# Attention phase of an AdaLN block: k projected from plain codes and scaled in place, softmax and v in fp16 halves, q's sine products swapped by transfers, instructions in a new order

## The reference

```python
def _dequant(codes, scales):                       # GS = 128: one scale per 128 input rows and output column
    w = codes.astype(jnp.float32) - 8.0
    return w * jnp.repeat(scales, GS, axis=0)

def _rope(x):
    ...
    re = xe * cos - xo * sin
    ro = xo * cos + xe * sin
q = hidden_states @ _dequant(q_codes, q_scales)
...
```

## Time and profile before

| | |
|---|---|
| time, median of 3 runs (lowest, highest) | 1821.96 us (1821.85, 1822.86) |
| the profiled execution's own time | 1821.32 us |
| its span | 1819.5 us, 34099 instructions |
| PE busy | 1767.9 us (97%) |
| PEld busy | 1019.7 us (56%) |
| DVE busy | 1378.0 us (76%) |
| ACT busy | 1223.1 us (67%) |
| POOL busy | 692.2 us (38%) |
| mean granted PE clock | 0.987 |

### The profile page before, as it was taken

How to read it: one execution, slowest core, us unless ns; L and a number is a source line. 1 busy time by engine, 2 the same in 40 slices (tenths; PEclk the granted TensorE clock), 3 DMA queues, 4 the chain that set the end, 5 groups by cost and what they waited for, 6 DMA issues and landing times. The chain is left out here.

```text
span 1819.5 us, 34099 instructions
## 1 busy us (share of the span) xinstructions
PE 1767.9 (97%) x14143; PEld 1019.7 (56%) x14143; DVE 1378.0 (76%) x2104; ACT 1223.1 (67%) x2090; POOL 692.2 (38%) x501
## 2 busy tenths in 40 slices
PE   8889999999999999999999999999999999689998
PEld 7845555555555555555555555555555555256665
DVE  4657777777777777777777777777777777389997
ACT  2257777777777777777777777777777777522222
POOL 1144334433443344334433443344333333133332
PEclk9999999999999999999999999999999999789999
DMA  6100010001000100010001000100000000412221
GB/s 252 38 33 24 12 36 1 24 13 36 1 24 13 36 1 24 13 36 1 24 13 36 1 24 13 36 1 24 13 1 2 1 1 1 151 47 74 79 82 47
DMA packets 24039, 58.70 MB, mean 32 GB/s; under 512 B 7256, under 2 KB 7768, under 8 KB 22608
## 3 DMA queue, kind: packets, MB, share of 16 engines
q1 hardware_dynamic: 23888, 56.55, 9.4%
HBM read 47.61 MB, written 8.93 MB: 31 GB/s over the span
## 5 line engine op out<-in xcount | busy, mean ns | idle before, releaser
L840 ACT ACTIVATE banks<-banks,ratios 128x512 f32<-128x512 f32 x768 | 476.1, 658 | 137.8 <-PE banks L612 137.4
L612 PE MATMUL banks<-o_hl,w_o 128*128 128x512 f16 x2048 | 532.2, 382 | 6.4 <-DVE o_hl L731 4.5
L536 PE MATMUL banks<-hT,w_q 128*128 128x512 f16 x2048 | 527.6, 380 | 7.3 <-DVE q_sin L688 4.0
L835 ACT ACTIVATE banks<-banks,ratios 128x512 f32<-128x512 f32 x768 | 492.8, 665 | 26.1 <-PE banks L536 15.4
L789 POOL TENSOR_TENSOR q_f<-q_f,q_sin 128x1024 f32<-128x1024 f32 x128 | 301.1, 2352 | 294.5 <-DVE q_sin L688 294.5
L612 PEld LDWEIGHTS banks<-o_hl,w_o 128*128 128x128 f16 x2048 | 187.4, 98 | 243.7 <-DVE accT L741 17.1
L688 DVE TENSOR_TENSOR q_sin<-banks,rope_q 64x1024 f32<-64x1024 f32 x256 | 312.8, 1222 | 13.3 <-POOL q_f L789 8.0
L536 PEld LDWEIGHTS banks<-hT,w_q 128*128 128x128 f16 x2048 | 191.6, 98 | 229.6 <-ACT banks L835 6.0
L845 ACT ACTIVATE o_hl<-banks 128x512 f16<-128x512 f32 x256 | 138.9, 595 | 144.8 <-PE banks L596 144.8
L741 DVE SCALAR_TENSOR_TENSOR accT<-banks,scales,accT 128x512 f32<-128x512 f32 x224 | 158.0, 746 | 60.8 <-PE banks L612 55.0
L563 PEld LDWEIGHTS banks<-w_kv,hT 128*128 128x128 f16 x3072 | 182.2, 98 | 30.1
(11 more groups left out here) (117 smaller groups left out, 1639.3 us busy)
## 6 DMA issues: line engine op xcount, KB each, us to landing
codes<-in_codes SPq DMA_DIRECT2D x40, 512.0 KB, 3.7
accT<-in_xT SPq DMA_DIRECT2D x8, 1024.0 KB, 12.3
x_f<-in_x SPq DMA_DIRECT2D x32, 256.0 KB, 3.0
out<-res SPq DMA_DIRECT2D x32, 256.0 KB, 2.1
kv_s<-in_kv_scales SPq DMA_DIRECT2D x8, 512.0 KB, 4.8
hT<-aggb_rows SPq DMA_DIRECT2D x1, 2048.0 KB, 12.8
hT<-in_base_T SPq DMA_DIRECT2D x1, 1024.0 KB, 5.9
aggw_rows<-agg_sb SPq DMA_DIRECT2D x1, 512.0 KB, 2.7
```

Of the source, the lines that this page charges most:

```text
L536: mm = pe.matmul(banks[:, tile], w_q[:, n[2], kt * RF * HD + tile * HD:kt * RF * HD + (tile + 1) * HD], hT[:, kt, hp, t0:t0 + CHUNK], star ...
L612: mm = pe.matmul(o_bank(t), w_o[:, p[2], h * D + tile * P:h * D + (tile + 1) * P], o_hl[:, op, h], start=h == 0 and op == 0, stop=op == 1, ...
L835: act.activation(banks[:, tile], banks[:, tile], ACT.Copy, scale=ratio(0, n, tile, kt)).then_inc(q_scaled[tile], 1)
L840: act.activation(o_bank(t), o_bank(t), ACT.Copy, scale=ratio(1, p, 2 * pair + t, h)).then_inc(o_scaled, 1)
```

## The change

- k's weights become plain codes minus 8 in fp16 (`make_k`: one POOL instruction where four were). `project_k` does 2 matmuls for a kt, 8 in all, and DVE multiplies `kv_bank` by the ratio in place between them (`scale_k`, 3 a step); the last scale is in the tables `rope_k`.
- `move_v` writes only the high fp16 half of v, and DVE writes the low one (`v_low`). The softmax is split as well: ACT writes the high half (`p_high`), POOL the low one (`p_low`), DVE transposes both in one instruction of 1024 fp16 elements. `values` does 3 fp16 matmuls where one f32 matmul was.
- `turn_sin` is one instruction of 128 partitions that leaves the products where they are. SP moves each half of the partitions to the other with two DMAs (`swap_q`) into a new tile `q_swap`, and `add_q` waits for them. `q_sin` and `q_swap` are single buffers, so the swap of one pair waits for the addition of the other.
- Every engine's order in `body` is rewritten; semaphores are split by tile or bank. SP issues one code piece a step (`load`) between the swaps.

The diff, cut to its core:

```diff
-    def make_kv(self, pool, g, which):
...
+    def make_k(self, pool, g):
+        self.wait_piece(pool, g, 0)
+        pool.tensor_scalar(self.k[:, g % 2], self.codes[:, 0, 0:KT * HD], -8.0, 1.0, ALU.add, ALU.mult)
...
+        def swap_q(n, pair):
+
+            sp.wait_ge(q_sin_done[pair], at(n) + 1)
+            if pair or at(n):
+
+                sp.wait_ge(q_ready[1 - pair], at(n) + pair)
+            for h in range(2):
+                sp.dma_start(q_swap[64 * h:64 * (h + 1)], q_sin[64 * (1 - h):64 * (2 - h)]).then_inc(q_swapped[pair], 16)
...
+        def body(n, i, p):
+            if n:
+                load(n)
+            if i:
+                swap_q(i, 1)
+            if n:
+                swap_q(n, 0)
...
+        def project_k(n, kt):
+            t0 = n[1] * CHUNK
+            if kt:
+                pe.wait_ge(k_scaled, 3 * at(n) + kt)
...
+            for hp in range(2):
+                mm = pe.matmul(kv_bank, w.k[:, n[2], kt * HD:(kt + 1) * HD], hT[:, kt, hp, t0:t0 + CHUNK],
+                               start=kt == 0 and hp == 0, stop=hp == 1, skip_group_check=True)
             mm.then_inc(k_psum, 1)
...
             for j in range(CT):
                 for b in (2 * half, 2 * half + 1):
-                    if half and j == 0:
-                        pe.wait_ge(out_ready, TB * at(i) + b - 1)
-                    mm = pe.matmul(o_bank(b)[:, j * P:(j + 1) * P], v_f[b * S:(b + 1) * S, i[1] % 2, j],
-                                   pT[b * S:(b + 1) * S, j * P:(j + 1) * P], start=True, stop=True, skip_group_check=True)
+                    rows = slice(b * S, (b + 1) * S)
+                    for m, (vp, pp) in enumerate(PASSES):
+                        mm = pe.matmul(o_bank(b)[:, j * P:(j + 1) * P], v_hl[rows, p[1] % 2, vp, j],
+                                       pT_hl[rows, pp, j * P:(j + 1) * P], start=m == 0, stop=m == 2, skip_group_check=True)
...
+        def scale_k(n, kt):
+            dve.wait_ge(k_psum, KT * at(n) + kt + 1)
+            dve.tensor_scalar(kv_bank, kv_bank, w.ratios[:, n[0], K_ROW, kt:kt + 1], None, ALU.mult).then_inc(k_scaled, 1)
...
         def turn_sin(n, pair):
+            if n[1] == 0 and n[0]:
+                dve.wait_ge(w_ready, n[0])
 
             if pair or at(n):
-                dve.wait_ge(q_ready[1 - pair], at(n) + pair)
-            for h in range(2):
-                ins = turn(n, pair, 1, slice(64 * (1 - h), 64 * (2 - h)), q_sin[64 * h:64 * (h + 1)])
-            ins.then_inc(q_products[pair], 1)
...
+                dve.wait_ge(q_swapped[1 - pair], 32 * (at(n) + pair))
+            turn(n, pair, 1, slice(0, P), q_sin[:]).then_inc(q_sin_done[pair], 1)
...
+            dve.transpose(pT_hl[:].rearrange("p a t -> p (a t)"), p_hl[:].rearrange("p a t -> p (a t)")).then_inc(probs_T, 1)
...
+        def v_low(n):
+            dve.wait_ge(v_hi, at(n) + 1)
+            hi, lo = (v_hl[:, n[1] % 2, part].rearrange("p j d -> p (j d)") for part in range(2))
+            dve.scalar_tensor_tensor(out=lo, in0=kv_bank, scalar=1 / WSCALE, in1=hi, op0=ALU.mult, op1=ALU.subtract).then_inc(v_ready, 1)
...
         def add_q(n, pair):
-            pool.wait_ge(q_products[pair], at(n) + 1)
+            pool.wait_ge(q_cos_done[pair], at(n) + 1)
+            pool.wait_ge(q_swapped[pair], 32 * at(n) + 32)
             q = q_f[:, 2 * pair:2 * pair + 2]
-            pool.tensor_tensor(q, q, q_sin[:], ALU.add).then_inc(q_ready[pair], 1)
+            pool.tensor_tensor(q, q, q_swap[:], ALU.add).then_inc(q_ready[pair], 1)
...
+        def p_low(i):
+            pool.wait_ge(p_hi, at(i) + 1)
+            pool.tensor_tensor(p_hl[:, 1], sc[:], p_hl[:, 0], ALU.subtract).then_inc(p_ready, 1)
...
+        def p_high(i):
+            act.wait_ge(probs, at(i) + 1)
+            act.activation(p_hl[:, 0], sc[:], ACT.Copy).then_inc(p_hi, 1)
```

More of the change, by code:

```diff
@@ L258, in _ @@
         sp.dma_start(aggb_rows, agg_sb[:, S * S:]).then_inc(agg_stored, 16)
-        w.load(sp, a, 0)
+        for j in range(PIECES):
+            w.load_piece(sp, a, 0, j)
         sp.wait_ge(agg_stored, 32)
@@ L583, in scores, with values @@
             mm.then_inc(scores_psum, 1)
-        def values(i, half):
+        def values(p, half):
             if half == 0:
-                pe.wait_ge(probs_T, at(i) + 1)
-                pe.wait_ge(v_ready, at(i) + 1)
-                if at(i):
-                    pe.wait_ge(acc_added, NT * at(i))
+                pe.wait_ge(probs_T, at(p) + 1)
+                pe.wait_ge(v_ready, at(p) + 1)
+                if at(p):
+                    for tile in (2, 3):
+                        pe.wait_ge(acc_added[tile], at(p))
+            else:
+                for b in range(2):
+                    pe.wait_ge(out_ready[b], at(p) + 1)
@@ L598, in values @@
                     if j == CT - 1:
-                        mm.then_inc(pv_psum, 1)
-        def output(p, pair, h):
-            if h == 0 and pair == 0:
-                pe.wait_ge(out_ready, TB * at(p) + TB)
-            for t in range(2):
-                tile = 2 * pair + t
-                if h:
-                    pe.wait_ge(o_scaled, 12 * at(p) + 6 * pair + 2 * (h - 1) + t + 1)
-                elif pair:
-                    pe.wait_ge(acc_added, NT * at(p) + t + 1)
-                for op in range(2):
-                    mm = pe.matmul(o_bank(t), w_o[:, p[2], h * D + tile * P:h * D + (tile + 1) * P], o_hl[:, op, h],
-                                   start=h == 0 and op == 0, stop=op == 1, skip_group_check=True)
-                mm.then_inc(o_psum, 1)
+                        mm.then_inc(pv_psum[half], 1)
@@ new lines, in output @@
+        def output(p, tile, h):
+            if h:
+                pe.wait_ge(o_scaled[tile], 3 * at(p) + h)
+            else:
+                for b in range(TB):
+                    pe.wait_ge(out_ready[b], at(p) + 1)
+                if tile >= 2:
+                    pe.wait_ge(acc_added[tile - 2], at(p) + 1)
+            for op in range(2):
+                mm = pe.matmul(o_bank(tile), w.o[:, p[2], h * D + tile * P:h * D + (tile + 1) * P], o_hl[:, op, h],
+                               start=h == 0 and op == 0, stop=op == 1, skip_group_check=True)
+            mm.then_inc(o_psum[tile], 1)
@@ L750, in body @@
             if i:
-                turn_sin(i, 1)
+                turn_cos(i, 1)
+                v_low(i)
             if p:
+                out_low(p, 3)
                 out_low(p, 2)
-                out_low(p, 3)
             if n:
-                rotate_k_sin(n)
+                scale_k(n, 0)
+            if i:
+                scores_T(i)
+            if n:
+                scale_k(n, 1)
             if i:
                 softmax_max(i)
+            if n:
+                scale_k(n, 2)
             if p:
+                add_out(p, 1)
                 add_out(p, 0)
-                add_out(p, 1)
+            if i:
+                softmax_sum(i)
             if n:
@@ L774, in body @@
             if p:
+                add_out(p, 3)
                 add_out(p, 2)
-                add_out(p, 3)
         program(body)
@@ L822, in body @@
                 normalize(i)
-                if i[0] < NKV - 1:
-                    dequantize(i)
+                p_low(i)
         program(body)
         pool.wait_ge(v_psum, STEPS)
+        for tile in range(RF):
+            pool.wait_ge(q_psum[tile], KT * STEPS)
         pool.memset(mixw_f, 0.0).then_inc(mixw_zeroed, 1)
```

390 lines of the change are left out of this document (218 added, 172 removed).

## The result

The changed kernel takes 1976.93 us (median of 4 runs, 1974.96 to 1979.53), the kernel before 1822.19 us (4 runs, 1821.85 to 1822.86). The ratio is 1.0853, with a 95% interval from 1.0839 to 1.0867. Predicted were 1787 us, with a range from 1762 to 1828.

The account below looks back on a forecast made before the run. The prediction took PE to be the bound, without holes. A step would go from 22.81 to 22.24 us; 63 steps give -36 us, the ends +2, so 1787 us, range 1762 to 1828.

Parts of the forecast that it names:

- Nearest: 2.7 ... so I take 2.7: loop 20.8, cover 1.4: Swap time taken from a 512 KB store out of SBUF, 2.7 us, giving a loop of 20.8 us with 1.4 cover.
- D: Time of one swap of q's sine products between partition halves, by two DMAs; taken as 2.7 us, bounds 2.1 to 3.7.
- 15.4 + 2D, hidden for D up to 3.4: Loop from one step's scores to the next's, through both swaps: 15.4 us plus 2D, hidden under the 22.24 us step.
- Rival 4: The swap loop is the bound, from D = 3.4; 1822 us at 3.7, 1860 at 4.0; chance 0.10.
- two slots for three matmuls: Values blocks on PE: fp16 matmuls of two sequences partly overlap, 1.10 us a block against the old 1.09, change 0.
- always two side by side: Lower bound for a values block on PE, row groups fully overlapping: 0.87 us, or -0.44 us a step.
- Rival 2: Values blocks on PE run fully side by side, -0.44 us a step: 1759 us; chance 0.08.
- Rival 3: Values on PE: fp16 blocks of 32 rows do not overlap, +0.90 us a step: 1845 us; chance 0.12.
- 4 x 0.2165 = 0.87: k on PE: 12 matmuls become 8, saving 0.87 us a step.
- Holes 0.3: Waits on PE in the new order, at output heads, scale_k, add_out and unseen places: 0.3 us a step.
- Rival 5: The new order opens more holes on PE, 0.7 instead of 0.3 us a step: 1813 us; chance 0.13.
- Ends +2: First step and end of the kernel, outside the steady steps: +2 us in all.

Follow-up runs that it names:

- e2_half_columns: The changed kernel with each swap DMA moving one of the pair's two tiles, half of the bytes: 1785.54 us.
- e4_filled_wait: The changed kernel with nine more mask matmuls on PE ahead of its wait in front of the scores: 1930.15 us.
- e10_no_transfer: The changed kernel without the swap transfers, the rotation add taking the sine product as it lies, other work the same: 1761.57 us.
- e7_values_f32: The kernel of e6_scores_later with the values part undone, one f32 matmul again and no v_low, p_high, p_low: 1818.40 us.
- the third pass: The kernel of e6_scores_later with a third matmul, with weights of zero, in each of a step's four k passes: 1811.10 us.
- e6_scores_later: The changed kernel reordered: last passes of q tiles 1 and 0, an output and a k pass ahead of the scores, turn_sin and scale_k ahead of scores_T: 1780.87 us.
- e9_two_queues: The changed kernel with the second DMA of each swap issued by ScalarE's queue, in time with the first: 2014.74 us.

## Why the prediction was wrong, step by step

**The step that failed: "Nearest: 2.7 ... so I take 2.7: loop 20.8, cover 1.4".** D was 4.35 us and 4.32 (medians; means 4.41 and 4.52). The bounds, 2.1 to 3.7, did not hold it either, so the range could not. The rows behind them were of one DMA each, with one end outside SBUF; the swap is two DMAs one behind the other, the second 0.50 later, and both move out of and into SBUF. Each row was a time to landing, and none of a pair. What the Trainium skill gives ("DMA: Bandwidth & Descriptors", Anatomy of one DMA), 2.0 us plus bytes / 436e3, is a fit for transfers that GpSimd issues, while SyncE issues these. As an estimate it agrees with the halved transfers (128 KB: 2.3 by both) and not with the full ones: 2.6 for the first 256 KB against 3.1, 3.2 for the pair against 4.2. The measurement decides.

**The loop, "15.4 + 2D, hidden for D up to 3.4".** The mechanism was right, and its size nearly so. Between 400 and 1400 us 22 steps of the changed kernel have the full clock. In each of them the step less its two D is 15.62 to 15.72 us, mean 15.64, though D goes from 4.2 to 5.5: the step follows both D one for one. With D = 3.2 (e2_half_columns) the step is 22.17, just above PE's 21.88. By the measured sizes the loop is hidden up to (21.88 - 15.64) / 2 = 3.1. Rival 4 had the right place and price (13 us for 0.1) and nearly the threshold, and a chance of 0.10 because its D ended at 4.0. By its own formula D = 4.35 gives 15.4 + 8.7 = 24.1 and 1821 + 63 x 1.29 + 2 = 1904 us. To the measured 1977 some 73 are missing. 0.24 us a step that the loop is longer are 15 of them, 0.23 that the mean D is above 4.35 are another 15, and the clock is some 41.

**Not in the prediction at all: the clock.** It took the full clock of the earlier trace rows for granted. It falls in some of the steps whose waits in front of the scores are 2.4 to 4.1 us long, and that costs some 41 us (0.64 us a step; e4_filled_wait, without it, is 47 us faster). Neither did the prediction have the swaps of 4.95 to 5.55 us, ten of 79. Only two of them have a code load beside them, and their cause stays open.

**PE's sum.** For each part, in us a step from start to start, what the prediction had, and what e10_no_transfer has over before (mask and scores, 1.32 in both, are left out of the rows but not of the step):

| part | before | predicted | measured | after |
|---|---|---|---|---|
| k | 2.60 | -0.87 | -0.54 | 2.06 |
| values | 2.18 | 0 | -0.62 | 1.56 |
| output | 6.92 | | +0.21 | 7.13 |
| v | 2.68 | | +0.10 | 2.78 |
| q | 7.10 | | -0.08 | 7.02 |
| holes, all parts | | +0.3 | in the rows above | |
| step | 22.81 | 22.24 | | 21.88 |

- **Values, "two slots for three matmuls".** Wrong, and on the safe side. 24 fp16 matmuls on 32 rows take 0.78 us, less than the 0.87 for "always two side by side", though the order is three and three. Rival 2's mechanism, with a chance of 0.08, is what happened; the undoing in e7_values_f32 confirms 0.62. Rival 3 (no overlap) is refuted.
- **k, "4 x 0.2165 = 0.87".** The matmuls went, but 0.33 us came back as waits beside the passes, and the third pass cost only 0.43. The prediction had put 0.05 on `scale_k` and 0.13 on `add_out`.
- **Holes 0.3.** They are 0.33 on k, 0.21 on the output and 0.10 on v, less 0.08 on q: 0.56. Rival 5's 0.7 was nearer than the 0.3 taken; as the values gained more, the sum came out lower than forecast.

Without D the prediction would have been 22.24 against 21.88 a step, 1787 against 1761.6 us, a hair below the range: two errors of opposite sign, 0.62 on the values and 0.26 on the holes, so even that nearness would have been luck in part. "Ends +2" can't be told from these runs.

**Where the expected gain went.** -60 us is there (e10_no_transfer), 215 are lost to the wait on the swaps, clock included. e6_scores_later has 41 of the 60 with the transfers in. What stays open: why the clock falls at some of the waits and not at others (once the wait was 3.4 us and it did not fall), what lengthens the ten swaps, and how much of the 19 us between e6_scores_later and e10_no_transfer another order could give; one attempt failed.

## What to carry to other kernels

Before work moves from an engine to a transfer, find the loop that it stands in from step to step, and count how often: D is paid as many times as the loop holds it, and costs little once its start no longer hangs on the loop's end: a few moved passes gave back 196 of 215 us. For a transfer that no row shows, count to the landing of the last of its DMAs and widen the upper bound well past the nearest row. A matmul taken away is worth its time only if the producer that its neighbours wait for is not the next bound: look at distances of starts on PE, not at its idle time.

## What the runs showed of the hardware

- A swap of two 256 KB halves within SBUF, 4 KB per partition, takes 4.2 us to the last landing, with one queue or two, when no other transfer runs beside it; the half that lands first takes 3.1. Two halves of 128 KB take 3.0 us to the add. With a code load of 512 KB issued 0.51 us behind the first DMA (e9_two_queues) the pair takes 5.3 us to the last landing; issued 1.15 us behind it, 4.3.
- fp16 matmuls on 32 rows and 128 columns on two row groups, three of one group and then three of the other, take 0.78 / 24 = 0.033 us each; those of v on all rows, one behind the other, 0.056.
- With a wait of 2.4 to 4.1 us in each step TensorE's granted clock is at half 17 times in 40 steps, for 3.4 us each; work without use in the wait (e4_filled_wait) keeps it at 1.00, and gained 47 us net.
